# A hybrid block of linear attention, experts and sparse attention: swapped halves by transfer, GpSimd's order, straight code

## The chip, the cores and the metric

One core of one Trainium2 chip. The time is the device time of one execution in microseconds (us); lower is better. Engines: TensorE (PE; its weight load is shown as PEld), VectorE (DVE), ScalarE (ACT), GpSimd (POOL), SyncE (SP), which here only issues transfers.

## The reference, cut to what matters

Sixteen images of 256 tokens, width 128, float32. Four blocks with a residual each: linear attention, top-1 of 8 experts, sparse attention, the same experts. The change is in the sparse attention, of which this matters:

```python
Q, K, V = jnp.split(x @ w_qkv.T + b_qkv, 3, axis=-1)
Q, K = (_rope(Q), _rope(K))   # [x1*cos - x2*sin, x1*sin + x2*cos], x1 and x2 the halves
iq, ik, iw = ...              # index queries (4 heads), index keys, head weights
head_scores = relu(einsum('bqhd,bkd->bhqk', iq, ik))
index_scores = einsum('bhqk,bqh->bqk', head_scores, iw)
_, top_idx = jax.lax.top_k(index_scores, 32)
logits = einsum('bqd,bkd->bqk', Q, K) * scale + attn_bias   # -inf off top_idx
attn_out = softmax(logits) @ V
```

## The kernel before, in words

Each engine has its own program; semaphores order them. Stage one is the linear attention. Then the tokens are sorted by expert: the routing tables are worked out, 32 gathers on GpSimd's queue (L425) bring the rows in order, and 39 incidences (tile, expert) pass through the experts (`experts_tensor`, `experts_scalar`, `experts_vector`). Then comes the sparse attention, then routing and experts a second time.

The sparse attention is a pipeline over the 16 images, one step per image, its order written out by hand on each engine. In step s:

- TensorE: transposes of the normalised image s (L689), eight projections in four pairs (`project`, L658 and L661): two of index queries, index keys, q, q with its halves swapped, k, k swapped, and V times the output weights. Between them the transposed probabilities of image s-2 (L668). Then the product of probabilities and V of image s-2 (L722), index scores of image s (L677), logits of image s-1 (L732).
- ScalarE: evicts the projections (`projected`, L886; `vb`, L889), exponentials of image s-2 (L899), `prT` (L908), the head weights `iw` (L913), the next image's normalisation `xb` (L862), relu of the index scores (`rel`, L925), the first two heads times their weights (`part`, L932), the penalty `pen` of image s-1 from what the top-k left (L942).
- GpSimd: rotation of q and k of image s, as products with cosine (L479) and sine (L481) of 128x512 each and their sum `qr` (L486); `add_heads` for each of the two chunks (`head_sum`, L464); `inverse_std(s)`, which adds eps and takes the power (L456, L458) and gives `rs`; the output bias onto `X` (L491); `gather_x(s+3)`, two indirect transfers (L445).
- VectorE: for image s-1 the third and fourth head's share of the index scores (L1272, L1278) for chunks 0 and 1, with the masked logits of image s-2 (L1286) between; then four rounds of max (L1327) and match_replace (L1330), and beside them the output normalisation `xf` (L1260), `nb` (L1235), the division `attended` (L1248), statistics (L1208, L1215), and behind the last round the aggregates (L1227), which give `mv`.
- SyncE: two stores of 128 KB for an image as soon as `xf` and `x` are there (`store_rows`).

The names of the counters: `mv` is counted up once in VectorE's step s (after two steps ahead of image 0), and `inverse_std(u)` waits for `mv >= u + 3`, that is for the aggregates of step u. `hs` counts head sums, and L1272 waits for `hs >= C*b + c + 1` with b = s-1. `pje` counts evicted projections, `rp` the rotation's products, `qr` the rotated pairs, `S` the logits.

In this stage, in ScalarE's and VectorE's expert stages, and in SyncE's programs the middle steps are hardware loops (`steps` and `incidences` with `Fori`), whose counts are worked out in registers. TensorE's expert stage and GpSimd's attention stage are written out. `alone` is a wait followed by an increment of a counter nobody waits for.

## Time and profile before

| | us |
|---|---|
| median of three runs (lowest, highest) | 610.64 (608.79, 612.69) |
| the profiled execution: own time, span | 614.45, 612.6 |
| busy in the span: PE, DVE, ACT, POOL | 456.6, 381.5, 338.0, 285.5 |
| windows: linear attention and first routing | 0 to 106 |
| first expert stage, with its gathers | 106 to 238 |
| sparse attention | about 250 to 455 |
| in 340 to 350: PE, DVE, ACT, POOL busy, PE's granted clock | 9.64, 9.40, 8.67, 7.67 of 10.00, 1.00 |
| in 440 to 450: the same | 5.16, 8.17, 3.06, 0.93 of 10.00, 0.67 |
| second routing and expert stage | 455 to 612 |

The times of the timeline count from the start of the span. The profiled execution is one run; its own time stands beside its span since a little lies around the span. A granted clock of 1.00 is TensorE's full 2.4 GHz, 0.50 is 1.2 GHz, and values between are mixtures over the window.

### The profile page before, as it was taken

To read this page: it belongs to the slowest core of one execution; us is meant where nothing else is said; L and a number is where in the kernel's file an instruction comes from. 1 tells how busy PE (TensorE), PEld (TensorE's weight loads), DVE (VectorE), ACT (ScalarE), POOL (GpSimd) and SP (SyncE) were. 2 spreads that over 40 slices of the span, in tenths; PEclk is the share of its full clock that TensorE was granted. 3 is DMA by queue.
4 is the path that set the end of the run, shared out by engine and by line. 5 is a ranking of instruction groups with operands and counts; after the bars stand their busy time and mean duration, and the time that the engine had idled before them with its cause. 6 is when DMAs were issued, how large, how long until landed. Compare 5 with 4: busy or idle time off the path is not lost. (4 is left out here: it accounts for less than half of the span.)

```text
span 612.6 us, 12728 instructions
## 1 busy us (share of the span) xinstructions
PE 456.6 (75%) x3048; PEld 395.4 (65%) x3048; DVE 381.5 (62%) x1502; ACT 338.0 (55%) x935; POOL 285.5 (47%) x329
## 2 busy tenths in 40 slices
PE   1889958611989886899899899989648402999882
PEld 1688848511889886666667667667438402889881
DVE  6789967001565662189899999999957001555561
ACT  1668821201566651688988998998520201566660
POOL 5654421774000003587778778785410773044442
PEclk9989977855999998799999999999757955898996
DMA  8912221332011111001101001100110332001010
GB/s 249 312 54 71 77 79 3 103 103 69 5 32 33 31 31 32 9 15 30 28 27 53 26 26 41 37 27 18 36 35 2 104 107 65 2 32 32 31 32 17
DMA packets 45061, 32.32 MB, mean 53 GB/s; under 512 B 13524, under 2 KB 39508, under 8 KB 45012
## 3 DMA queue, kind: packets, MB, share of 16 engines
q1 hardware_dynamic: 39892, 19.11, 11.1%
q0 software_dynamic: 5120, 12.62, 7.5%
q8 instruction: 23, 0.38, 0.3%
q14 instruction: 26, 0.21, 0.1%
HBM read 19.10 MB, written 12.62 MB: 52 GB/s over the span
## 5 line engine op out<-in xcount | busy, mean ns | idle before, releaser
L637 PE MATMUL bank<-WE,hT 128*128 x624 | 90.9, 292 | 45.9 <-issue 27.8
L637 PEld LDWEIGHTS bank<-WE,hT 128*128 128x128 f32 x624 | 82.5, 206 | 48.8 <-issue 48.8
L627 PE MATMUL bank<-X,w 128*128 x624 | 89.0, 288 | 30.1 <-issue 29.3
L627 PEld LDWEIGHTS bank<-X,w 128*128 128x128 f32 x624 | 80.6, 202 | 33.5 <-issue 33.2
L1177 DVE TENSOR_SCALAR hT<-bank,w 128x128 f32<-128x128 f32 x156 | 47.6, 347 | 69.5 <-issue 35.6
L832 ACT ACTIVATE X<-bank 128x128 f32 (+1 forms) x64 | 17.8, 278 | 117.8 <-PE bank L618 66.0
L425 POOL DMA_INDIRECT big<-rows,gidx x64 | 61.0, 953 | 46.5 <-DVE gidx L1145 27.6
L445 POOL DMA_INDIRECT X<-x,pidx x32 | 31.6, 989 | 98.2 <-DMA x<-big 90.6
L658 PE MATMUL bank<-xbT,WB 128*128 128x256 f32 x224 | 63.0, 416 | 12.7 <-ACT xbT L870 8.8
L845 ACT ACTIVATE hT<-bank,w 128x128 f32<-128x128 f32 x156 | 48.6, 365 | 30.4 <-issue 17.2
L837 ACT ACTIVATE w<-WE 128x644 f32 x78 | 57.4, 736 | 4.3 <-DVE big L1189 3.7
L431 POOL DMA_INDIRECT out<-big,gidx x32 | 31.1, 972 | 59.9 <-DVE big L1189 59.4
L658 PEld LDWEIGHTS bank<-xbT,WB 128*128 128x128 f32 x224 | 41.9, 203 | 25.5 <-ACT iq L886 9.5
L1330 DVE MATCH_REPLACE8 wk<-m,wk 128x256 f32<-128x256 f32 x128 | 51.4, 410 | 0.0
L1183 DVE TENSOR_TENSOR yb<-bank,w 128x128 f32<-128x128 f32 x78 | 22.6, 289 | 44.7 <-remote 26.9
L1327 DVE MAX8 m<-wk 128x8 f32<-128x256 f32 x128 | 47.6, 413 | 0.0
L677 PE MATMUL bank<-ik,iq 64*128 64x256 f32 x256 | 38.0, 402 | 0.7 <-ACT big L925 0.7
L464 POOL TENSOR_TENSOR head_sum<-big 128x256 f32<-128x256 f32 x32 | 23.8, 743 | 29.7 <-ACT big L932 29.6
L1189 DVE SCALAR_TENSOR_TENSOR big<-yb,gm,big 128x128 f32 x78 | 27.5, 353 | 16.1 <-DVE yb L1183 11.4
L925 ACT ACTIVATE big<-bank 128x512 f32<-128x512 f32 x64 | 34.6, 591 | 1.1 <-PE bank L677 1.0
L512 PE MATMUL bank<-cst 128*128 128x128 f32 x188 | 28.1, 323 | 2.5 <-DVE big L1189 2.5
L886 ACT ACTIVATE big<-bank,COL 128x256 f32<-128x256 f32 x64 | 29.3, 492 | 1.1 <-PE bank L658 0.7
(163 smaller groups left out, 1032.1 us busy)
## 6 DMA issues: line engine op xcount, KB each, us to landing
WE<-w_experts SPq DMA_DIRECT2D x2, 2048.0 KB, 11.3
rows<-xf SPq DMA_DIRECT2D x32, 128.0 KB, 2.2
rows<-X SPq DMA_DIRECT2D x32, 128.0 KB, 2.5
X<-x SPq DMA_DIRECT2D x4, 512.0 KB, 6.5
x<-big SPq DMA_DIRECT2D x32, 64.0 KB, 1.5
big<-rows,gidx POOLq DMA_INDIRECT x64
WB<-w_idx SPq DMA_DIRECT2D x1, 640.0 KB, 5.2
WE<-b SPq DMA_DIRECT2D x1, 512.0 KB, 12.6
```

Source lines behind the costliest of these rows:

```text
L425: pool.indirect_dma_start(xg[:, j, :], None, rows_dram[n], bass.IndirectOffsetOnAxis(ap=gidx[:, j:j + 1], axis=0)).then_inc(f["g"][j % G_R ...
L445: pool.indirect_dma_start(X[:, t, :], None, x2_dram, bass.IndirectOffsetOnAxis(ap=pidx[:, t:t + 1], axis=0)).then_inc(b_["x"][r], 16)
L627: mm = pe.matmul(bank[r + 2 * (k // 2)][:, k % 2 * P:(k % 2 + 1) * P], w1[st.slot(1, 4)][:, k * P:(k + 1) * P], moving, start=True, stop=True)
L637: mm = pe.matmul(bank[4 + r][:, 0:D], hT[r][:, k, :], WE[:, bass.ds(expert[(s - 2) % TURN], 1), W2_AT + k * D:W2_AT + (k + 1) * D].rearran ...
L658: mm = pe.matmul(to, WB[:, i * D:(i + 1) * D], xbT[r][:, :], start=True, stop=True)
L677: mm = pe.matmul(bank[h % 2][:, h // 2 * S:(h // 2 + 1) * S], iq[r][lo:lo + IDX_DIM, h // 2, c * P:(c + 1) * P], ik[r][lo:lo + IDX_DIM, :] ...
L837: act.activation(w1[st.slot(0, 4)][:, :], WE[:, bass.ds(expert[st.base], 1), 0:W1_LEN].rearrange("p a w -> p (a w)"), ACT.Copy).then_inc(f ...
L845: act.activation(hT[r][:, k, :], bank[r][:, k * P:(k + 1) * P], ACT.Relu, bias=w1[st.slot(1, 4)][:, B1_AT + k:B1_AT + k + 1]).then_inc(f[" ...
L925: act.activation(rel[r][:, c, i::2, :], bank[i][:, :].rearrange("p (h k) -> p h k", h=2), ACT.Relu).then_inc(b_["rel"], 1)
L1177: dve.tensor_scalar(hT[r][:, k, :], bank[2 + r][:, k % 2 * P:(k % 2 + 1) * P], w1[st.slot(1, 4)][:, B1_AT + k:B1_AT + k + 1], 0.0, ALU.add ...
L1327: dve.max(m8[:, c, :], wk[r][:, c, :]).then_inc(b_["v"], 1)
L1330: dve.match_replace(wk[r][:, c, :], m8[:, c, :], wk[r][:, c, :], NEG).then_inc(b_["v"], 1)
```

## The change

Four things. The projections with swapped halves go: TensorE makes six instead of eight per image (index queries, index keys and q, k and V), in three pairs that alternate between two banks, and ScalarE evicts two fewer. SyncE copies the halves instead: after k is evicted, two transfers within SBUF write `qk[:, 0:2]` with upper and lower 64 partitions exchanged into `qk[:, 2:4]`. GpSimd's step has a new order: cosine product (into `qr`), `inverse_std(s)`, bias, gathers, head sum 0, wait for the transfers, sine product, sum, head sum 1. All loops named above but those of the linear attention and SyncE's first two are written out as straight code, and `alone` with a constant is only a wait. The weight table and the bias columns lose the swapped copies.

```diff
 def alone(eng, sem, count, passed):
-    if not isinstance(count, int) or count > 0:
+    if isinstance(count, int):
+        after(eng, sem, count)
+    else:
         eng.wait_ge(sem, count)
         eng.sem_inc(passed, 1)
...
         def incidences(eng, lag):
-            yield from (Step(s) for s in range(HEAD))
-            with eng.Fori(0, (T - HEAD) // TURN) as turn:
-                for k in range(TURN):
-                    yield Step(HEAD + k, TURN, turn)
-            yield from (Step(s) for s in range(T, NT + lag))
+            yield from (Step(s) for s in range(NT + lag))
...
-            for st in steps(sp, B, 0, 4, 2):
-                store_rows(1, st, 0, lambda b, r: X[:, tiles(b), :])
+            def turn_halves(b, r):
+                sp.wait_ge(b_["pje"], 6 * b + 5)
+                after(sp, b_["qr"], b - 1)
+                for lo in (0, P // 2):
+                    hi = P // 2 - lo
+                    sp.dma_start(qk[r][lo:lo + P // 2, 2:4, :], qk[r][hi:hi + P // 2, 0:2, :]).then_inc(b_["turn"][r], 16)
+            for st in (Step(s) for s in range(B + 4)):
+                if st.on(0, B):
+                    turn_halves(st.item(0), st.slot(0, 2))
+                if st.on(4, B):
+                    store_rows(1, st, 4, lambda b, r: X[:, tiles(b), :])
...
             for s in range(B + 2):
                 b, r = s, s % 2
                 if b < B:
-                    pool.wait_ge(b_["pje"], 8 * b + 7)
-                    pool.tensor_tensor(qk[r][:, 0:2, :], qk[r][:, 0:2, :], const("cos").unsqueeze(1).to_broadcast([P, 2, S]),
+                    pool.wait_ge(b_["pje"], 6 * b + 5)
+                    after(pool, b_["S"], C * (b - 1))
+                    pool.tensor_tensor(qr[r][:, :, :], qk[r][:, 0:2, :], const("cos").unsqueeze(1).to_broadcast([P, 2, S]),
                                        ALU.mult).then_inc(b_["rp"], 1)
-                    pool.tensor_tensor(qk[r][:, 2:4, :], qk[r][:, 2:4, :], const("sin").unsqueeze(1).to_broadcast([P, 2, S]),
-                                       ALU.mult).then_inc(b_["rp"], 1)
-                    add_heads(b, r, 0)
-                    pool.wait_ge(b_["rp"], 2 * (b + 1))
-                    after(pool, b_["S"], C * (b - 1))
-                    pool.tensor_tensor(qr[r][:, :, :], qk[r][:, 0:2, :], qk[r][:, 2:4, :], ALU.add).then_inc(b_["qr"], 1)
-                    add_heads(b, r, 1)
                 inverse_std(s)
...
                 if b + 3 < B:
                     gather_x(b + 3)
+                if b < B:
+                    add_heads(b, r, 0)
+                    pool.wait_ge(b_["turn"][r], 32 * (b // 2 + 1))
+                    pool.tensor_tensor(qk[r][:, 2:4, :], qk[r][:, 2:4, :], const("sin").unsqueeze(1).to_broadcast([P, 2, S]),
+                                       ALU.mult).then_inc(b_["rp"], 1)
+                    pool.wait_ge(b_["rp"], 2 * (b + 1))
+                    pool.tensor_tensor(qr[r][:, :, :], qr[r][:, :, :], qk[r][:, 2:4, :], ALU.add).then_inc(b_["qr"], 1)
+                    add_heads(b, r, 1)
```

On TensorE (the loops of ScalarE and VectorE are written out likewise):

```diff
-            for st in steps(pe, B, 4, 6, 2, ahead=1):
+            for st in (Step(s) for s in range(B + 4)):
...
-                    after(pe, b_["pje"], 8 * b + 2 * (pair - 1))
+                    after(pe, b_["pje"], 6 * b + 2 * (pair - 1))
...
-                        to = bank[2 + pair % 2][:, i % 2 * S:(i % 2 + 1) * S]
+                        to = bank[2 + (3 * st.slot(0, 2) + pair) % 2][:, i % 2 * S:(i % 2 + 1) * S]
...
                     project(1)
-                    project(2)
                 if st.on(2, B):
...
                     turn_probabilities(b, r, 0)
                 if st.on(0, B):
-                    project(3)
+                    project(2)
```

On ScalarE:

```diff
                 if st.on(0, B):
-                    projected(2)
+                    projected(2, (0,))
...
                 if st.on(0, B):
-                    projected(3)
-                    act.wait_ge(b_["pj"], 5 * (b + 1))
+                    projected(2, (1,))
+                    act.wait_ge(b_["pj"], 4 * (b + 1))
```

## Rows read from the trace of the kernel before

**Rows 1.** Timeline, ScalarE: start us, length us, line, tile, count, idle before.

```profile
345.13 0.60 ACT L908 ACTIVATE prT<-bank 128x512 f32<-128x512 f32 x1 [0.42 <-issue]
...
345.63 0.47 ACT L886 ACTIVATE big<-bank,COL 128x256 f32<-128x256 f32 x1
...
346.98 0.39 ACT L889 ACTIVATE vb<-bank 128x256 f32<-128x256 f32 x1 [0.88 <-PE bank L722]
...
358.75 0.39 ACT L889 ACTIVATE vb<-bank 128x256 f32<-128x256 f32 x1 [0.89 <-PE bank L722]
```

**Rows 2.** Timeline, TensorE, the same step.

```profile
344.63 0.38 PE L668 MATMUL bank<-cst,lg 128*128 128x128 f32 x2
...
345.79 1.16 PE L722 MATMUL bank<-vb,prT 128*128 128x128 f32 x8
```

**Rows 3.** Timeline, VectorE, one step.

```profile
330.06 0.48 DVE L1272 SCALAR_TENSOR_TENSOR wk<-big,iw,head_sum 128x256 f32<-128x256 f32 x1
330.45 0.48 DVE L1278 SCALAR_TENSOR_TENSOR wk<-big,iw,wk 128x256 f32<-128x256 f32 x1
...
331.19 0.80 DVE L1278 SCALAR_TENSOR_TENSOR wk<-big,iw,wk 128x256 f32<-128x256 f32 x1
331.91 0.74 DVE L1327 MAX8 m<-wk 128x8 f32<-128x256 f32 x2
...
340.16 0.38 DVE L1227 BATCH_NORM_AGGREGATE mv<-stat 128x2 f32<-128x6 f32 x4
340.86 0.91 DVE L1272 SCALAR_TENSOR_TENSOR wk<-big,iw,head_sum 128x256 f32<-128x256 f32 x1 [0.32 <-issue]
```

**Rows 4.** Timeline, GpSimd, one step.

```profile
338.40 0.72 POOL L464 TENSOR_TENSOR head_sum<-big 128x256 f32<-128x256 f32 x1 [1.57 <-ACT big L932]
339.08 1.27 POOL L486 TENSOR_TENSOR qr<-big 128x512 f32<-128x512 f32 x1
...
341.44 0.39 POOL L456 TENSOR_TENSOR vpe<-mv,eps 128x4 f32<-128x4 f32 x1
341.91 1.05 POOL L458 TENSOR_TENSOR rs<-vpe,mhalf 128x4 f32<-128x4 f32 x1
342.94 0.72 POOL L491 TENSOR_TENSOR X<-X,bo_bc 128x256 f32<-128x256 f32 x1
343.83 1.04 POOL L445 DMA_INDIRECT X<-x,pidx  x1 [0.17 <-issue]
345.17 0.95 POOL L445 DMA_INDIRECT X<-x,pidx  x1 [0.30 <-issue]
```

**Rows 5.** Page, DMA issues: count, KB each, us to landing.

```profile
rows<-xf SPq DMA_DIRECT2D x32, 128.0 KB, 2.2
```

**Rows 6.** Timeline, VectorE and GpSimd, start of the attention stage.

```profile
242.99 0.25 DVE L1227 BATCH_NORM_AGGREGATE mv<-stat 128x2 f32<-128x6 f32 x2
...
243.32 0.20 POOL L456 TENSOR_TENSOR vpe<-mv,eps 128x2 f32<-128x2 f32 x1 [1.93 <-DVE mv L1227]
243.59 0.73 POOL L458 TENSOR_TENSOR rs<-vpe,mhalf 128x2 f32<-128x2 f32 x1
```

**Rows 7.** Timeline, ScalarE, GpSimd and VectorE, first image.

```profile
252.01 1.35 ACT L886 ACTIVATE big<-bank,COL 128x256 f32<-128x256 f32 x3 [0.71 <-PE bank L658]
...
259.00 0.78 POOL L464 TENSOR_TENSOR head_sum<-big 128x256 f32<-128x256 f32 x1
...
259.82 0.48 DVE L1272 SCALAR_TENSOR_TENSOR wk<-big,iw,head_sum 128x256 f32<-128x256 f32 x1 [0.62 <-POOL head_sum L464]
```

**Rows 8.** Timeline, VectorE and TensorE, last image and tail.

```profile
436.25 0.48 DVE L1272 SCALAR_TENSOR_TENSOR wk<-big,iw,head_sum 128x256 f32<-128x256 f32 x1
...
449.88 2.07 PE L722 MATMUL bank<-vb,prT 128*128 128x128 f32 x8 [0.69 <-ACT prT L908]
```

**Rows 9.** Page, DMA queues; and timeline, VectorE, second expert stage.

```profile
q8 instruction: 23, 0.38, 0.3%
...
504.42 0.29 DVE L1183 TENSOR_TENSOR yb<-bank,w 128x128 f32<-128x128 f32 x1 [16.19 <-remote]
```

More of the change, by code:

```diff
@@ L282, in build @@
                "idx", "rel", "prt", "hs", "s1", "wk", "v", "pen", "S", "ttr", "exp", "PT", "prT", "PV",
-               "pinv", "xo")} | {"x": sems("b_x", 2)}
+               "pinv", "xo")} | {"x": sems("b_x", 2), "turn": sems("b_turn", 2)}
         def xrows(dram, b, lo, hi):
@@ L589, in route_tensor @@
                     pe.wait_ge(b_["row"], 1)
[L590 to L591 removed]
+                    pe.matmul(bank[3][:, 0:D], bv_rep[:, :], WB[:, 5 * D:6 * D], start=True, stop=True)
+                    pe.matmul(bank[4][:, 0:D], WB[:, 6 * D:7 * D], WB[:, 5 * D:6 * D], start=True, stop=True).then_inc(b_["wvo"], 1)
                 keep_clock(KEEP_ROUTE, bank[2][:, 0:P])
@@ L712, in _ @@
                         mm = pe.matmul(bank[5][:, S + c * IDX_HEADS:S + (c + 1) * IDX_HEADS], xbT[r][:, c * P:(c + 1) * P],
-                                       WB[:, 9 * D:9 * D + IDX_HEADS], start=False, stop=(c == C - 1))
+                                       WB[:, 7 * D:7 * D + IDX_HEADS], start=False, stop=(c == C - 1))
                     mm.then_inc(b_["pj"], 1)
@@ L800, in _ @@
                     xf_out(0, st.item(5), st.slot(5, 2), bank[6][:, 0:S])
-            act.activation(bv_rep[:, :], ones, ACT.Copy, scale=COL[:, 9:10]).then_inc(b_["row"], 1)
+            act.activation(bv_rep[:, :], ones, ACT.Copy, scale=COL[:, 7:8]).then_inc(b_["row"], 1)
             def route_exp(n, k):
@@ L873, in _, with projected @@
             turned(0, 0)
-            for st in steps(act, B, 4, 6, 2, ahead=1):
+            for st in (Step(s) for s in range(B + 4)):
                 b, r = st.item(0), st.slot(0, 2)
-                def projected(pair):
-                    act.wait_ge(b_["pj"], 5 * b + pair + 1)
-                    for i in (2 * pair, 2 * pair + 1):
-                        src = bank[2 + pair % 2][:, i % 2 * S:(i % 2 + 1) * S]
+                def projected(pair, which=(0, 1)):
+                    act.wait_ge(b_["pj"], 4 * b + pair + 1)
+                    for i in (2 * pair + w for w in which):
+                        src = bank[2 + (3 * r + pair) % 2][:, i % 2 * S:(i % 2 + 1) * S]
                         if i == 3:
-                            after(act, b_["qr"], b - 1)
-                        if i < 7:
-                            dst = iq[r][:, i, :] if i < 2 else ik[r][:, :] if i == 2 else qk[r][:, (0, 2, 1, 3)[i - 3], :]
+                            after(act, b_["rp"], 2 * (b - 1))
+                        if i < 5:
+                            dst = iq[r][:, i, :] if i < 2 else ik[r][:, :] if i == 2 else qk[r][:, i - 3, :]
                             act.activation(dst, src, ACT.Identity, bias=COL[:, 2 + i:3 + i]).then_inc(b_["pje"], 1)
@@ L1267, in _ @@
             shifts(Step(0), 0)
-            for st in steps(dve, B, 3, 6, 2, ahead=2):
+            for st in (Step(s) for s in range(B + 3)):
                 def add_third(c):
@@ L1352 @@
     wt = a["L0_attn_b_w_qkv"].T
-    other = np.r_[D // 2:D, 0:D // 2]
     wiq, wik = a["L0_attn_b_w_iq"].T, a["L0_attn_b_w_ik"].T
@@ L1356 @@
     wiw[:, :IDX_HEADS] = a["L0_attn_b_w_iw"].T
-    w_idx = np.concatenate([wiq, wik, wik, wt[:, :D], wt[:, :D][:, other], wt[:, D:2 * D], wt[:, D:2 * D][:, other],
-                            a["L0_attn_b_w_o"].T, a["L0_attn_b_w_qkv"][2 * D:], wiw], axis=1)
+    w_idx = np.concatenate([wiq, wik, wik, wt[:, :D], wt[:, D:2 * D], a["L0_attn_b_w_o"].T, a["L0_attn_b_w_qkv"][2 * D:], wiw], axis=1)
     bq, bk, bv = np.split(a["L0_attn_b_b_qkv"], 3)
@@ L1361 @@
     cols = np.stack([a["L0_attn_a_gamma"].reshape(D), a["L0_attn_a_beta"].reshape(D), biq[:D], biq[D:],
-                     np.concatenate([bik, bik]), bq, bq[other], bk, bk[other], bv], axis=1)
+                     np.concatenate([bik, bik]), bq, bk, bv], axis=1)
     w1 = a["L0_ffn_W1"].transpose(1, 0, 2)
```

9 lines of the change are left out of this document (4 added, 5 removed).

## The prediction

> **What bounds the kernel now.** The view by windows puts the sparse-attention stage at about 250 to 455 us, with TensorE at full clock in most of it (the small table above). Its 16 images run as a pipeline, one step per image, so I read one step engine by engine in the timeline, looking for what each engine waits for. ScalarE evicts `vb` at 346.98 and again at 358.75: a step is 11.8 us. In it ScalarE stands still twice, for the turned probabilities (start 345.13) and for 0.88 us before `vb`, which waits for TensorE's product of probabilities [rows 1]. TensorE in turn reaches that product at 345.79 only after the transpose at 344.63, and ScalarE must evict that first [rows 2]. So the loop is ScalarE's queue with this piece of TensorE's in it, 11.8 us long. VectorE is the near rival: from its third product for chunk 1 (330.06) to the end of the statistics (340.16 + 0.38 = 340.54) it is hardly ever idle [rows 3]. GpSimd has slack, but its place in the order matters below: it makes both head sums of image s (the first at 338.40), and only then the inverse deviations (341.44, 341.91), the bias sum (342.94) and the two gathers (343.83, 345.17) [rows 4]. The inverse deviations wait for `mv`, which VectorE gives at the very end of its step s, behind all four rounds of max and match.
>
> **Part by part.**
>
> *Two projections fewer.* Each image loses two 128x256 products on TensorE and two evictions on ScalarE; one of these is the 0.47 us at 345.63 [rows 1]. Both evictions lie in the gaps where ScalarE waits for TensorE anyhow. The eviction of k now waits for the V product, so `prT` could come about 0.1 us later. On the old loop this is worth -0 to +0.1 us a step, and that loop is no longer the bound (below). I take 0.
>
> *The transfers.* SyncE issues two of 128 KB (64 partitions of 2 KB each) for each image once k is evicted. The nearest row is the store of one image, 128 KB, 2.2 us from issue to landing [rows 5]. The sine product comes some 13 us after k's eviction in the new order (below), so they are hidden; they would show only above 13 us. On SyncE's queue the store of image s-4 now stands behind k of image s. Its data are ready before that and its buffer is wanted again only in the next step: nothing. At the tail the stores go without any transfer ahead of them.
>
> *GpSimd's order.* Now: cosine product, inverse deviations(s), bias sum, gathers, head sum 0, sine product, sum, head sum 1. The head sums of image s, which VectorE needs for the first operations of its step s+1, thus stand behind a wait for `mv` from the end of VectorE's step s. Before, they stood ahead of that wait. This closes a ring: VectorE's whole step, then GpSimd's whole chain, then VectorE's next step. Nothing overlaps any more except the cosine product. What queues behind the wait on GpSimd is everything listed; who waits for it is VectorE (third product), and through it ScalarE and TensorE.
>
> The ring, from rows. VectorE: third product of chunk 1 at 330.06 to the end of the aggregates at 340.54, 10.48 us. The fourth product of chunk 1 took 0.80 us there, with GpSimd running, and its sister 0.48; the max followed 0.72 us after its start, where 0.40 is the pitch of the uncontended ones. GpSimd will be idle at that point, so minus 0.32: **10.16 us** [rows 3]. From `mv` to GpSimd's start: 242.99 + 0.25 = 243.24 to 243.32, 0.08 us [rows 6]. GpSimd: from 341.44 to the end of the second gather 345.17 + 0.95 + about 0.05, 4.73 us; head sum 0.68 (the pitch 338.40 to 339.08); sine product 1.27 (as the sum of the same shape at 339.08) plus 0.07 for a wait on its own result (243.32 + 0.20 to 243.59 [rows 6]); sum 1.27 less 0.03 of overlap; head sum 0.72: **8.71 us** [rows 4]. Hand-over to VectorE, from 259.00 + 0.78 to 259.82: 0.04 us [rows 7]. Sum 10.16 + 0.08 + 8.71 + 0.04 = **19.0 us a step**, where it was 11.8.
>
> There are 15 such turns between the third product of chunk 1 of the first image and that of the last. Ten (s = 3 to 12) are full: 190.0. Three (13 to 15) have no gather, 2.34 less: 16.7; the last two of them also have two-column deviations (0.5 less) and less statistics (estimated at 0.5): 15.7 each. Turn 1 has no divide, no `xf`, half of the statistics (estimated at 2.1 from the lengths of the like) and narrow deviations: 16.4. Turn 2 lacks `xf`, 0.6: 18.4. Sum 190.0 + 16.7 + 2 x 15.7 + 16.4 + 18.4 = 272.9 us.
>
> Its start: k of image 0 is evicted at about 252.5 (the fifth product, the first of the three at 252.01 [rows 7], instead of the seventh), the cosine product ends at 253.8, then 4.3 us of the narrow chain, 0.7, 1.3, 1.2, 0.7: VectorE starts at 262.0, against 259.82 [rows 7]. So it reaches the last image's third product at 262.0 + 272.9 = 534.9, before at 436.25 [rows 8]: **+98.7 us**. Behind it the tail runs as before.
>
> *Is another ring longer?* With 19 us a step TensorE works less than half of the time, and in the tail of before it stood at half clock, the product of probabilities taking 2.07 instead of 1.16 us [rows 2, 8]. With these lengths I followed ScalarE and TensorE from VectorE's masked logits: that product ends 5 to 6 us behind, VectorE wants it at 6.8; both parts of the head sums are there by 14 us, GpSimd asks for them at 15 and 18.3. So a low clock costs 0 here; from a delay of 1 us more it would begin to show.
>
> *Straight code.* In the old loop VectorE lost 0.32 us at each return, seen at 340.86 [rows 3]. In the attention stage this now lies inside its wait: 0. In each of the two expert stages VectorE has three turns: at most 2 x 2 x 0.32 = -1.3 us, and about -0.6 if half is hidden behind TensorE. `alone` loses an increment; max follows max at the pitch of other instructions, so 0. Against this, more instructions must be brought in: the instruction queues moved 23 packets in one of them before, and during the gathers ahead of the experts VectorE stood for 16.19 us with nothing in the trace to show for it [rows 9]. If that is code coming in behind the gathers, more code could lengthen it; if not, nothing. Bounds -1.3 and +20; I take -1, since the work at that place was straight code already.
>
> *The skill, weighed.* [Rows 3] show a product with two inputs in SBUF at 0.48 us alone and 0.80 to 0.91 beside GpSimd. The Trainium skill, SBUF — State Buffer, "SBUF: two separate sides", says that VectorE and GpSimd share one port pair as an exclusive lock; the trace agrees, and by it the new order even saves VectorE that much, the 0.32 us taken off above. The Trainium skill, Runtime: NRT & Kernel Launch, "Instruction fetch mechanics", says that a branch taken out of the two pages at hand forces a fetch, and so speaks for straight code; the row shows 0.32 us at a return, so by the trace there is little to win.
>
> **Forecast.** The profiled execution took 614.45 us, 3.8 above the median of 610.64, which I start from: 610.6 + 98.7 - 1 = 708 us.
>
> **Rivals.**
> 1. *A second ring or slow code adds to it.* The low clock makes the products late by more than the 1 us of slack, or code arrives late on VectorE or behind the gathers. For: the stalls of [rows 9] and the half clock of [rows 8]. Price: 1 to 2 us in 15 turns, or 5 to 20 once: 720 to 745. Chance 0.17.
> 2. *The ring is shorter.* Operations on GpSimd or VectorE that were slowed by each other run faster now, or my estimate of the start is late: 0.5 to 1.5 us a turn, 685 to 698. For: only VectorE's two-input operations show contention in the rows; GpSimd's lengths are all alike. Chance 0.12.
> 3. *Not slower.* It decides at one point: whether `mv` of step s is there before GpSimd needs it. If GpSimd ran a whole step behind, its wait would be over when it comes to it, and ScalarE's ring would stay: 11.8 + 0.1 a step with the stage's two fewer products, 610 us, or 600 if ScalarE's gaps closed. Against it: VectorE cannot start step s+1 without head sums s, and these stand behind `mv` s, so nobody can be ahead. Chance 0.02, half of it faster.
> 4. *The transfer is the bound.* It would need more than 13 us against 2.2 [rows 5]; each us beyond adds 15: 725 for one. Chance 0.02.
>
> The forecast itself (699 to 718) has 0.67. Below 692 or above 730 I leave some 0.15, so the range is 692 to 730. The three runs of before spread by 0.6%, so about 1% is what a measurement can tell. Faster 0.01, same 0.01, slower 0.98.
>
> **What would show it.** VectorE's third product waits about 8 us for `head_sum` in each step, and GpSimd's deviations wait for `mv`, with GpSimd going from them through gathers and head sums without a gap; step length 19.0 us, 16.7 or less in the last three; the sine product waits for no transfer; ScalarE and TensorE idle for some 9 us a step, TensorE's granted clock falls. Wrong would be a step of 12 us, a wait of VectorE for ScalarE instead, or a sine product that waits for DMA. The expert stages should keep their length within 2 us each.

## The result and the profile after

The changed kernel takes **704.06 us** (median of 4 runs, 702.65 to 704.28), the kernel before 611.66 (4 runs beside them, 608.79 to 613.18): ratio 1.151, with an interval of 1.146 to 1.156. It is 15% slower. The profiled execution took 703.98 us with a span of 702.2; that of before took 614.45 with 612.6.

VectorE in one step of the attention stage, from the timeline of the changed kernel (start, length, line, tile, idle before). It answers to [rows 3].

```profile
379.45 0.38 DVE L1238 BATCH_NORM_AGGREGATE mv<-stat 128x2 f32<-128x6 f32 x4
385.27 1.40 DVE L1283 SCALAR_TENSOR_TENSOR wk<-big,iw,head_sum 128x256 f32<-128x256 f32 x1 [5.44 <-POOL head_sum L473]
...
388.51 0.48 DVE L1283 SCALAR_TENSOR_TENSOR wk<-big,iw,head_sum 128x256 f32<-128x256 f32 x1 [1.50 <-POOL head_sum L473]
...
391.49 1.00 DVE L1271 TENSOR_SCALAR xf<-X,mv,rs 128x128 f32<-128x128 f32 x2
...
398.51 0.38 DVE L1238 BATCH_NORM_AGGREGATE mv<-stat 128x2 f32<-128x6 f32 x4
```

Where [rows 3] ran on from the aggregates into the next step, VectorE now stands for 5.44 us, works for some 1.8, and stands for 1.50 more, both times for a head sum. The third product of chunk 1 starts at 388.51 and in the neighbouring steps at 369.45 and 407.57: **a step is 19.06 us**.

GpSimd in the same step, the answer to [rows 4]:

```profile
379.91 0.20 POOL L465 TENSOR_TENSOR vpe<-mv,eps 128x4 f32<-128x4 f32 x1 [6.81 <-DVE mv L1238]
380.19 1.05 POOL L467 TENSOR_TENSOR rs<-vpe,mhalf 128x4 f32<-128x4 f32 x1
381.23 0.71 POOL L494 TENSOR_TENSOR X<-X,bo_bc 128x256 f32<-128x256 f32 x1
382.11 1.04 POOL L454 DMA_INDIRECT X<-x,pidx  x1 [0.17 <-issue]
383.45 0.95 POOL L454 DMA_INDIRECT X<-x,pidx  x1 [0.30 <-issue]
384.43 0.73 POOL L473 TENSOR_TENSOR head_sum<-big 128x256 f32<-128x256 f32 x1
385.11 1.27 POOL L501 TENSOR_TENSOR big<-big,cst 128x512 f32<-128x512 f32 x1
386.46 1.33 POOL L504 TENSOR_TENSOR qr<-qr,big 128x512 f32<-128x512 f32 x1
387.75 0.72 POOL L473 TENSOR_TENSOR head_sum<-big 128x256 f32<-128x256 f32 x1
390.88 1.27 POOL L489 TENSOR_TENSOR qr<-big,cst 128x512 f32<-128x512 f32 x1 [2.41 <-ACT big L897]
```

It begins 0.08 us behind the aggregates (379.83) and runs from `vpe` to the second head sum with no idle time but the gathers' own; 0.04 us behind that head sum (388.47) VectorE starts. Each engine waits while the other works. The sine product (385.11) waits for no transfer.

The view that adds up the waits, from 240 to 540 us: who waited for whom, us in total, times, the longest.

```profile
DVE wk L1283 <- POOL head_sum L473: 106.9, 32, 9.7
POOL vpe L465 <- DVE mv L1238: 101.9, 15, 7.5
...
ACT lg L910 <- DVE lmin L1297: 69.3, 29, 5.2
POOL qr L489 <- ACT big L897: 38.5, 15, 4.9
```

The first two are the ring, seen from its two ends: 106.9 us of VectorE's (9.7 and 1.8 of them before the first turn) and 101.9 of GpSimd's. ScalarE's and TensorE's waits are the ring's echo. On the page, the granted clock and the transfers:

```profile
PEclk9999869559999996688777797776795595589997
...
big<-big SPq DMA_DIRECT2D x32, 128.0 KB, 2.4
```

The transfers land in 2.4 us, near the 2.2 of the stores in [rows 5]. In the attention stage the clock is below 0.8 of full speed in most slices, and in most steps TensorE's product of probabilities shows the length that it has at the half clock, as in [rows 8], where [rows 2] have 1.16:

```profile
392.44 2.06 PE L732 MATMUL bank<-vb,prT 128*128 128x128 f32 x8
```

It cost nothing: VectorE never waited for it, and the step in which this product took 1.14 us (410.96) is 19.05 us long all the same.

**Where the 89.6 us of span come from.** Cut both timelines at two points, the aggregates of the first image and the last third product of chunk 1.

| | before | after | difference |
|---|---|---|---|
| start to the first image's `mv` | 249.20 | 244.15 | -5.05 |
| from there to the last third product | 187.05 | 287.67 | +100.6 |
| from there to the end | 176.35 | 170.38 | -6.0 |

So the ring cost 100.6 us and everything outside it gave back 11.0. These are two single executions; the other pair of traces, b0 and a0 below, gives +102.0 and -5.4. From the first third product of chunk 1 (257.46) to the last (531.82) are 274.4 us in 15 turns; the last three turns, which have no gather, took 16.5, 15.6 and 15.5.

### The profile page after: what moved, and what is told of

Read it like the earlier page. It is cut to its first block and busy times, and to the rows that moved or that the text cites. A ratio compares the mean times of both kernels' runs of the same rounds, so it can differ in the third digit from the quotient of the medians.

```text
span 702.2 us, 11429 instructions
## 1 busy us (share of the span) xinstructions
PE 481.4 (69%) x2984; PEld 410.7 (58%) x2984; DVE 391.7 (56%) x1501; ACT 330.5 (47%) x902; POOL 284.9 (41%) x329
## 5 line engine op out<-in xcount | busy, mean ns | idle before, releaser
L648 PE MATMUL bank<-WE,hT 128*128 x624 | 87.9, 286 | 47.4 <-issue 35.0
L1283 DVE SCALAR_TENSOR_TENSOR wk<-big,iw,head_sum 128x256 f32<-128x256 f32 x32 | 31.3, 978 | 106.9 <-POOL head_sum L473 106.9
L679 PE MATMUL bank<-cst,lg 128*128 128x128 f32 x64 | 20.0, 415 | 76.8 <-ACT lg L910 76.8
L843 ACT ACTIVATE X<-bank 128x128 f32<-128x128 f32 x64 | 17.8, 279 | 115.2 <-PE bank L629 87.7
L856 ACT ACTIVATE hT<-bank,w 128x128 f32<-128x128 f32 x156 | 48.6, 366 | 27.3 <-issue 17.5
L679 PEld LDWEIGHTS bank<-cst,lg 128*128 128x128 f32 x64 | 8.6, 189 | 87.0 <-issue 69.3
L669 PE MATMUL bank<-xbT,WB 128*128 128x256 f32 x160 | 49.6, 448 | 9.9 <-ACT xbT L881 9.8
L465 POOL TENSOR_TENSOR vpe<-mv,eps 128x4 f32<-128x4 f32 (+1 forms) x20 | 4.1, 206 | 118.0 <-DVE mv L1238 118.0
L688 PE MATMUL bank<-ik,iq 64*128 64x256 f32 x256 | 48.2, 497 | 4.5 <-ACT big L936 4.5
L910 ACT ACTIVATE lg<-lg,lmin 128x256 f32<-128x256 f32 x32 | 16.3, 511 | 70.9 <-DVE lmin L1297 70.9
L669 PEld LDWEIGHTS bank<-xbT,WB 128*128 128x128 f32 x160 | 32.6, 222 | 15.9 <-ACT xbT L881 12.0
## 6 DMA issues: line engine op xcount, KB each, us to landing
WE<-w_experts SPq DMA_DIRECT2D x2, 2048.0 KB, 11.7
```

The costliest lines, as they stand in the source:

```text
L648: mm = pe.matmul(bank[4 + r][:, 0:D], hT[r][:, k, :], WE[:, bass.ds(expert[(s - 2) % TURN], 1), W2_AT + k * D:W2_AT + (k + 1) * D].rearran ...
L669: mm = pe.matmul(to, WB[:, i * D:(i + 1) * D], xbT[r][:, :], start=True, stop=True)
L688: mm = pe.matmul(bank[h % 2][:, h // 2 * S:(h // 2 + 1) * S], iq[r][lo:lo + IDX_DIM, h // 2, c * P:(c + 1) * P], ik[r][lo:lo + IDX_DIM, :] ...
L856: act.activation(hT[r][:, k, :], bank[r][:, k * P:(k + 1) * P], ACT.Relu, bias=w1[st.slot(1, 4)][:, B1_AT + k:B1_AT + k + 1]).then_inc(f[" ...
L1283: dve.scalar_tensor_tensor(wk[r][:, c, :], rel[r][:, c, 2, :], iw[r][:, c, 2:3], head_sum[r][:, c, :], ALU.mult, ALU.add).then_inc(b_["s1" ...
```

## The experiments

**Three things could explain the 100 us**: the order on GpSimd that makes head sums wait for `mv` (my theory), the transfers (a rival), or a second ring through ScalarE and TensorE (a rival). And the 11 us given back called for tests of their own. Kernels of one group ran on one chip beside runs of the kernel before. The chips are not alike: on two of them (groups 1 and 2) the kernel before takes 537 us, on the others 611. Only ratios, and differences within a group, are compared below; the absolute times in the expectations of e1, e2, e3 and e5 were meant for the slower chips. All the kernels compute the whole reference. In the diffs a minus is the changed kernel and a plus the experiment, unless it is said otherwise.

**Group 1** (before: 537.19, 23 runs): e1, e2, e4, e7. **Group 2** (before: 537.51, 17 runs): e3, e5, e6.

### e1: the old order of head sums, all else changed

GpSimd's whole second half goes back behind the second head sum; transfers, six projections and straight code stay.

```diff
-                inverse_std(s)
-                ... bias sum ...
-                    gather_x(b + 3)
                 if b < B:
                     add_heads(b, r, 0)
                     ... sine product, sum ...
                     add_heads(b, r, 1)
+                inverse_std(s)
+                ... bias sum ...
+                    gather_x(b + 3)
```

> The changed kernel with GpSimd's old order: cosine product, head sum 0, wait for the transfers, sine product, sum, head sum 1, and only then the inverse deviations, the bias and the gathers. Transfers, six projections and straight code stay. Theory of the ring (VectorE's step and GpSimd's chain in series, because the head sums stand behind the wait for mv): the step falls from 19.06 to 11.8 to 12.0 us and the time to 603 to 610 us. Rival, that the transfers or the waits for them cost the time: it stays above 690 us. A smaller form of it: the transfer now has no work in front of it but one head sum, and each us of waiting that shows on VectorE adds 16 us.

**536.10 us, ratio 0.997** (0.994 to 1.000). The whole loss is gone with the transfers still there. Most steps are 11.96 us long, some 12.2 to 14.1 (from one eviction of `vb` to the next, as in e6 and e8 to e10). Two losses that the kernel before did not show in this form, from VectorE's timeline:

```profile
304.03 2.20 DVE L1271 TENSOR_SCALAR xf<-X,mv,rs 128x128 f32<-128x128 f32 x2
...
359.36 0.49 DVE L1219 BATCH_NORM_STATS2 stat<-X 128x6 f32<-128x128 f32 x2 [1.52 <-DMA X<-x,pidx]
```

GpSimd in those two steps, and then SyncE in the second:

```profile
303.89 0.95 POOL L454 DMA_INDIRECT X<-x,pidx  x1 [0.30 <-issue]
304.87 1.27 POOL L489 TENSOR_TENSOR qr<-big,cst 128x512 f32<-128x512 f32 x1
...
352.97 1.04 POOL L454 DMA_INDIRECT X<-x,pidx  x1 [0.17 <-issue]
354.31 0.95 POOL L454 DMA_INDIRECT X<-x,pidx  x1 [0.30 <-issue]
```

```profile
353.39 1.15 SPq L367 DMA_DIRECT2D big<-big  x2
354.58 0.59 SPq L340 DMA_DIRECT2D rows<-xf  x1
```

`xf`, 0.59 us long in the kernel before, where only a gather runs beside it (345.31 beside 345.17 of [rows 4]), started 0.14 us into a gather and ended 0.09 us behind the cosine product that followed. And the rows of a gather issued at 354.31 were waited for until 359.36, with the transfers' packets and the store's issued around them. e9 and e10 take these two apart.

### e2: one line moved back

Of the new order, only the inverse deviations return to the end.

```diff
-                inverse_std(s)
                 if b < B:
                     pool.wait_ge(b_["xb"], b + 1)
                     ... bias sum, gathers, head sums, sine product, sum ...
+                inverse_std(s)
```

> The changed kernel with one call moved: the inverse deviations go behind head sum 1; bias and gathers stay in front of head sum 0 and the sine product. If the ring is closed by the wait for mv alone, this one line gives everything back: step 11.8 to 12.0 us, 603 to 610 us. If it is the quantity of work in front of the sine product (bias and two gathers, 3.2 us) that costs, the time stays some 45 us above the kernel before, 650 us or more.

**538.42 us, ratio 1.001** (0.999 to 1.004). Bias sum and gathers still stand ahead of the head sums, and the loss is gone all the same. So the ring is closed by **one wait**, that of the deviations for `mv`. GpSimd's timeline, where `vpe` no longer waits at all:

```profile
340.79 0.72 POOL L473 TENSOR_TENSOR head_sum<-big 128x256 f32<-128x256 f32 x1
341.47 0.39 POOL L465 TENSOR_TENSOR vpe<-mv,eps 128x4 f32<-128x4 f32 x1
...
344.80 1.27 POOL L489 TENSOR_TENSOR qr<-big,cst 128x512 f32<-128x512 f32 x1 [1.81 <-ACT big L897]
```

A step is 12.27 us, 0.45 over the old one; two are longer, 14.1 and 13.2 (more on them under e10). In most, `xf` takes 1.79 us (345.04 to 346.83) beside the cosine product and the bias sum, 1.2 more than alone.

### e3: the order alone, in the kernel before

Eight projections, both halves on TensorE, loops as before; only the order on GpSimd is the new one (a minus is the kernel before).

```diff
-                    ... sine product, head sum 0, sum, head sum 1 ...
                 inverse_std(s)
                 ... bias sum, gathers ...
+                if b < B:
+                    add_heads(b, r, 0)
+                    ... sine product, sum ...
+                    add_heads(b, r, 1)
```

> The kernel before with GpSimd's new order alone: cosine product, inverse deviations, bias, gathers, head sum 0, sine product, sum, head sum 1; eight projections, no transfers, loops as before. Theory of the ring: step 19 to 19.2 us and 700 to 712 us, since nothing else of the change is on that ring. Rival, that the slowdown needs the transfers or the straight code: 612 to 620 us.

**635.32 us, ratio 1.181** (1.176 to 1.187): +98 us from the order alone, with no transfer in the kernel. A step is 18.8 us. The two ends of the ring, on GpSimd:

```profile
384.66 0.20 POOL L456 TENSOR_TENSOR vpe<-mv,eps 128x4 f32<-128x4 f32 x1 [5.22 <-DVE mv L1228]
...
392.49 0.72 POOL L464 TENSOR_TENSOR head_sum<-big 128x256 f32<-128x256 f32 x1
...
397.01 1.27 POOL L479 TENSOR_TENSOR big<-big,cst 128x512 f32<-128x512 f32 x1 [3.79 <-ACT big L887]
```

The chain is 8.55 us (384.66 to 393.21), as in the changed kernel. The cosine product comes later here, behind eight projections, and so does not meet `xf`, which takes 0.59 us (at 396.23), 0.41 less than in the changed kernel: enough for the difference between 18.8 and 19.06.

### e5: a smaller dose

The deviations stay ahead of the head sums, bias sum and gathers go behind them.

```diff
                 inverse_std(s)
-                ... bias sum, gathers ...
                 if b < B:
                     add_heads(b, r, 0)
                     ... sine product, sum ...
                     add_heads(b, r, 1)
+                ... bias sum, gathers ...
```

> The dose: the changed kernel with the inverse deviations alone in front of head sum 0; bias and gathers go behind head sum 1. The ring stays closed but is shorter by bias and gathers: 10.38 us of VectorE, 0.08, then 0.28 + 1.04 + 0.68 + 1.35 + 1.29 + 0.72 = 5.36 us of GpSimd, 0.04: 15.9 us a step where it is 19.06, and 704 - 13 x 3.2 - 3 x 0.7 = 660 us. If the order mattered otherwise than by such a sum, the step would be 12 or 19 us.

**598.71 us, ratio 1.114** (1.109 to 1.119). The ring is there with a shorter chain on GpSimd:

```profile
393.69 0.20 POOL L465 TENSOR_TENSOR vpe<-mv,eps 128x4 f32<-128x4 f32 x1 [6.83 <-DVE mv L1238]
...
398.33 0.72 POOL L473 TENSOR_TENSOR head_sum<-big 128x256 f32<-128x256 f32 x1
...
402.20 1.29 POOL L489 TENSOR_TENSOR qr<-big,cst 128x512 f32<-128x512 f32 x1
```

From 393.69 to 399.05 are 5.36 us, 3.2 less than in the changed kernel, as the sum of the moved rows had it. The step averages some 16.6 us where I had expected 15.9 (in time, 61 us lost where my 660 us stood for 48): the chain is right, and VectorE's part is 0.76 too long. Of that, 0.32 is `xf` at 1.32 us instead of 1.00, beside the cosine product (402.20), and 0.45 the third product at 399.08, which took 0.93 beside the bias sum where [rows 3] have 0.48.

### e4: the straight code alone

The kernel before with the loops written out and with `alone` as a plain wait for a constant count, and nothing else (a minus is the kernel before; `alone` and the like lines of TensorE, ScalarE and SyncE are not shown).

```diff
-            yield from (Step(s) for s in range(HEAD))
-            with eng.Fori(0, (T - HEAD) // TURN) as turn:
-                for k in range(TURN):
-                    yield Step(HEAD + k, TURN, turn)
-            yield from (Step(s) for s in range(T, NT + lag))
+            yield from (Step(s) for s in range(NT + lag))
...
-            for st in steps(dve, B, 3, 6, 2, ahead=2):
+            for st in (Step(s) for s in range(B + 3)):
```

> The kernel before with straight code alone, projections and order as they were. By my prediction the loops cost 0.32 us at a return of VectorE, most of it hidden: 0 to -2 us. What the changed kernel's trace suggests: it ran 2.3 us less up to the attention stage and 5.5 us less behind it, and if straight code is the cause this kernel is 6 to 9 us faster than before, with the attention step unchanged at 11.8 us. If those 8 us came by chance from run to run, or from something else in the change, it stays within 2 us of before.

**528.11 us, ratio 0.983** (0.979 to 0.986): 9.1 us gained, where my sum had 1. It is the fastest of all versions. Its attention steps are 11.82 us long, as before.

### e7: e2 with the experts in loops again

The first hunk of e4's diff, the other way round, applied to e2. So e2 against e7 is the experts' straight code alone.

> As the kernel with the deviations last, but ScalarE's and VectorE's expert stages are hardware loops again. If straight code in the expert stages is what saves the 8 us outside the attention stage, this one is 5 to 9 us slower than the kernel with the deviations last; if not, they are within 2 us of each other.

**544.26 us, ratio 1.014** (1.009 to 1.018), 5.8 us over e2. From the first to the last weight row of the experts the two stages take 79.6 and 78.1 us with loops, 76.4 and 76.0 without: 5.3 of the 5.8. VectorE at such a turn, first in e2, then in e7:

```profile
143.36 0.16 DVE L1180 TENSOR_TENSOR gm<-big,mine 128x1 f32<-128x1 f32 x1 [2.16 <-PE bank L638]
143.50 0.61 DVE L1188 TENSOR_SCALAR hT<-bank,w 128x128 f32<-128x128 f32 x2
```

```profile
144.18 0.16 DVE L1184 TENSOR_TENSOR gm<-big,mine 128x1 f32 x1 [2.49 <-PE bank L642]
144.46 0.61 DVE L1192 TENSOR_SCALAR hT<-bank,w 128x128 f32<-128x128 f32 x2
```

With the loop VectorE starts its first operation 0.33 us later, and then 0.14 more pass before its second. The view puts the wait down to TensorE, but in e7 TensorE had long been done with this product:

```profile
142.65 1.06 PE L642 MATMUL bank<-X,w 128*128 x8
```

It ends at 143.71, 0.47 us before VectorE starts; in e2 the two are 0.14 us apart. So the delay is **VectorE's own**, 0.47 us to its second operation where [rows 3] show 0.32. With three turns in each stage the 5.3 us are 0.9 a turn on average, but they are not alike. Against the same weight rows of e2, ScalarE falls behind by 0.4, 0.5 and 2.2 us at the three turns of the first stage and by 0.5, 0.8 and 0.5 at those of the second. At the one of 2.2 us TensorE's clock fell as well, to 0.62 from 164 to 166 us; the product that takes 1.15 us at the same place in e2 took 1.83:

```profile
164.17 1.83 PE L642 MATMUL bank<-X,w 128*128 x8
```

In e3, which has the same loops, the clock stays full there, and this third turn costs 0.7 us. So a turn costs 0.4 to 0.8 us, and the rest of e7's loss, some 1.5 us, is this fall of the clock.

### e6: the third pair of projections ahead of the transposes

e2, with `project(2)` back at its old place on TensorE (a minus is e2).

```diff
                     project(0)
                     project(1)
+                    project(2)
                 ... turn_probabilities(b, r, 0) ...
-                if st.on(0, B):
-                    project(2)
```

> The kernel with the deviations last, and on TensorE the third pair of projections (k and V) in front of the first transposes of the probabilities instead of behind them. It tests what bounds the step when the ring is open: by my reading ScalarE waits for the transposes and then for the product of probabilities, and TensorE stands idle before them. If so, prT comes up to 0.8 us earlier, the step falls from 11.9 to 11.0 to 11.3 us, and the time by 8 to 13 us against the kernel with the deviations last. If VectorE is already the bound, it stays within 3 us of it.

**534.91 us, ratio 0.994** (0.991 to 0.998), some 4 us better than e2 by the two ratios to the kernel before; I had expected 8 to 13. Steps are 11.8 us with two at 12.5 to 12.65, and `xf` is still long (1.43). The step fell by 0.47 us against e2, and 0.36 of that is `xf`, at 1.43 instead of 1.79, since the cosine product now starts earlier. The eviction of k that came late was a part of what kept e2 back, and less than half of what I had counted on.

**Group 3** (before: 611.52, 23 runs): a0, b0, e8, e9; and **e10** on one more chip (before: 611.14, 17 runs). It asks two things: whether the results hold where the kernel before takes 611, and why no version with six projections gets past 0.994.

### a0 and b0: the changed kernel and the kernel before, again

> The changed kernel itself, on the chip of the experiments, where the kernel before takes 537 us and not 611. The ring has no part in what differs between the chips: steps of 19.06 us again, so 537 + 98.7 less 5.8 to 9 for straight code = 627 to 632 us. If the slowdown were a factor of the whole (1.151), it would be 618 us, and the steps shorter.

**706.1 us, ratio 1.150** (1.144 to 1.157). The absolute number that I had expected was that of the faster chips; it ran on one of the others. The ratio is that of the result, and steps are 19.06 us again:

```profile
387.36 1.40 DVE L1283 SCALAR_TENSOR_TENSOR wk<-big,iw,head_sum 128x256 f32<-128x256 f32 x1 [5.43 <-POOL head_sum L473]
...
390.60 0.48 DVE L1283 SCALAR_TENSOR_TENSOR wk<-big,iw,head_sum 128x256 f32<-128x256 f32 x1 [1.50 <-POOL head_sum L473]
```

> The kernel before itself, for its trace on this chip. Two accounts of the 74 us by which it is faster here: if TensorE's clock or all engines are faster, the attention step is shorter than 11.8 us; if it is the standing still of all engines behind the 32 gathers at the start of each expert stage, the step is 11.8 us as before, each expert stage is 35 to 38 us shorter, and no wait of 10 us without a cause stands in it.

**612.31 us** (one run). Its attention steps are 11.8 us, as on the faster chips; the difference is in the expert stages, 115.2 and 118.5 us long here, 78.3 and 79.8 in e3, which has the same loops and ran on a faster chip. VectorE behind the first stage's gathers:

```profile
134.42 0.29 DVE L1183 TENSOR_TENSOR yb<-bank,w 128x128 f32<-128x128 f32 x1 [14.23 <-remote]
...
152.68 0.61 DVE L1177 TENSOR_SCALAR hT<-bank,w 128x128 f32<-128x128 f32 x2 [17.32 <-issue]
```

These stand beside the 16.19 us of [rows 9]. In e3 and e4, on the faster chips, no such wait is found. The 37 and 39 us in the two stages account for all of the 74 us between the chips. So my question whether more code would lengthen those waits has an answer: not by anything seen. The same VectorE waits are 9.21 and 20.80 us in the trace of before and 8.51 and 21.17 in that of after, and the stages are shorter after (113.4 and 113.0) than before (115.9 and 118.2).

### e8: `xf` on ScalarE

e6, with the normalised output computed by ScalarE from a bias that VectorE prepares; it relieves VectorE's queue (a minus is e6).

```diff
-                for c in range(C):
-                    ins = dve.tensor_scalar(xf[r][:, c, :], one_tile(b, c), mv2[u][:, C + c, 0:1],
-                                            rs2[u][:, C + c:C + c + 1], ALU.subtract, ALU.mult)
+                dve.scalar_tensor_tensor(nbx[r][:, :], mv2[u][:, C:2 * C, 0], -1.0, rs2[u][:, C:2 * C],
+                                         ALU.mult, ALU.mult).then_inc(b_["nbx"], 1)
...
+                        ins = act.activation(xf[e][:, c, :], X[:, d * C + c, :], ACT.Identity,
+                                             scale=rs2[u][:, C + c:C + c + 1], bias=nbx[e][:, c:c + 1])
```

> The kernel with the third pair of projections first, and xf of the output side made by ScalarE behind prT, with a 0.15 us product on VectorE for its bias. There xf took VectorE 1.43 us a step beside GpSimd's cosine product. If VectorE's queue, with this wait for the shared port in it, bounds the step of 11.8 us, the step falls to 11.0 to 11.4 us and the time by 5 to 12 us, to 523 to 530 us. If ScalarE's ring bounds it, the 0.8 us added there fill its wait of 1.31 us before vb and the step stays at 11.8 us or grows by up to 0.3.

**609.92 us, ratio 0.996** (0.993 to 1.000), no better than e6. ScalarE's timeline:

```profile
340.31 0.60 ACT L919 ACTIVATE prT<-bank 128x512 f32<-128x512 f32 x1
341.62 0.88 ACT L928 ACTIVATE xf<-X,nbx,rs 128x128 f32<-128x128 f32 x2 [0.71 <-DVE nbx L1280]
342.40 0.36 ACT L900 ACTIVATE vb<-bank 128x256 f32<-128x256 f32 x1
```

ScalarE now does the 0.88 us of work and waits 0.71 for the bias, which VectorE makes no sooner: its tiny operation takes 0.60 to 0.79 us beside the cosine product, where the like one behind it (`nb`, 341.51) takes 0.15. Steps are 11.8 to 12.7, but for one of 13.5. That VectorE's queue as such bounds these versions is not borne out: relieving it moved the wait.

### e9: the cosine product later

e1, with the cosine product waiting for V's eviction too, so that it starts behind `xf`.

```diff
-                    pool.wait_ge(b_["pje"], 6 * b + 5)
+                    pool.wait_ge(b_["pje"], 6 * b + 6)
```

> The kernel with the old order of GpSimd, transfers and six projections (536.1 us), with one number changed: the cosine product waits for the eviction of V's product too and so starts behind VectorE's xf. If the collision of these two costs the 8 us by which that kernel is behind the one with straight code alone (528.1 us), xf takes 0.59 us in every step, the steps are 11.8 us throughout and the time is 528 to 532 us. If the transfers cost them by making the gathers land late, the waits of VectorE for gathered rows stay and so do 534 to 538 us.

**609.17 us, ratio 0.994** (0.991 to 0.998). `xf` is 0.59 us in every step, with a gather still beside it (353.62), so its 2.2 us in e1 did come from the cosine product. Yet steps are 11.7 to 12.5: seven of them wait for gathered rows, as here.

```profile
353.75 0.59 DVE L1271 TENSOR_SCALAR xf<-X,mv,rs 128x128 f32<-128x128 f32 x2
...
371.05 0.49 DVE L1219 BATCH_NORM_STATS2 stat<-X 128x6 f32<-128x128 f32 x2 [1.25 <-DMA X<-x,pidx]
```

The traces say more on this wait. In e4, with the same place of the gathers in GpSimd's order and no transfers, VectorE reads the rows 3.45 to 3.81 us behind the issue of the last gather and waits for them for 0.26 us at most. The twelve waits of e1 and e9 are up to 1.66 us, and but for one they end 3.8 to 5.2 us behind it; in ten of them the trace shows the transfers issued 0.8 to 1.0 us ahead of that gather. So the rows come late where transfers and gathers meet, which is argued from these rows and not from a run of its own.

### e10: the gathers first of all

TensorE as in e6; GpSimd: bias sum, gathers, cosine product (behind V's eviction), head sum 0, sine product, sum, head sum 1, deviations.

```diff
-                ... cosine product (for pje >= 6 * b + 5) ...
-                inverse_std(s)
                 if b < B:
                     ... bias sum ...
                 if b + 3 < B:
                     gather_x(b + 3)
                 if b < B:
+                    pool.wait_ge(b_["pje"], 6 * b + 6)
+                    ... cosine product ...
                     add_heads(b, r, 0)
                     ... sine product, sum, head sum 1 ...
+                inverse_std(s)
```

> Drawn from the others: the third pair of projections first on TensorE, and GpSimd in the order bias, gathers, cosine product (behind the eviction of V's product and so behind xf), head sum 0, sine product, sum, head sum 1, deviations last. No ring through mv, the gathers early enough, xf at 0.59 us. If the wait for the shared port was what held the step at 11.8 us, it falls to 11.3 to 11.6 us and the ratio to the kernel before to 0.97 to 0.98, as good as straight code alone (0.983) or better. If the chain of head sums, masked logits and exponentials bounds it, or TensorE's clock falls for want of work, the step is 11.8 to 12.1 us and the ratio 0.985 to 0.995.

**606.47 us, ratio 0.993** (0.991 to 0.996). No gather is late, since each is issued a whole step ahead of where e9 has it, and `xf` is 0.59 us; steps are 11.8 in part and 12.0 to 12.66 in the rest. What is left is seen in the view by windows (us; busy time of each engine; granted clock, DMA share, GB/s), here e10:

```profile
300.00:320.00 20.00, 17.58 (x100) 13.06 (x100) 19.34 (x80) 15.04 (x43) 14.88 (x16) 0.91 0.25 67
320.00:340.00 20.00, 17.12 (x103) 12.97 (x104) 18.01 (x75) 16.95 (x47) 16.71 (x18) 1.00 0.14 35
```

and the same stretches of e4, with eight projections:

```profile
300.00:320.00 20.00, 18.51 (x115) 14.15 (x115) 19.30 (x82) 17.37 (x50) 15.54 (x17) 1.00 0.17 41
320.00:340.00 20.00, 17.93 (x108) 13.99 (x110) 18.70 (x77) 17.39 (x50) 16.53 (x19) 1.00 0.15 37
```

Over 280 to 380 us TensorE is busy for 17.5 of 20 us in e10 and 18.1 in e4; the granted clock is full in all five windows of e4, and in e10 it is 0.91 in two and 0.96 in one. Step by step the falls of the clock can be priced. In three steps of e10 the product of probabilities takes 2.06, 1.39 and 1.80 us where it takes 1.14 in the others, here the last of them:

```profile
363.07 1.80 PE L730 MATMUL bank<-vb,prT 128*128 128x128 f32 x8
```

From third product to third product these three steps last 13.17, 12.76 and 13.18 us, 3.7 us over 11.8 each; all 15 steps take 178.45 us in e10 and 174.59 in e4. In size, the falls of the clock account for nearly all by which e10 is behind e4 in this stage. The long steps of e2 (product 2.05 us) and e6 (1.76) are of the same kind. No such step stands in e4 or in the kernel before (its last images left out), and none in e9, which has six projections too: there the clock is full in all five windows with TensorE busy for 16.2 of 20 us. So less work on TensorE does not by itself bring the fall; what does is open. What bounds the open ring at 11.8 us in e4 as in the kernel before was not changed by any of these edits, and is not settled.

## Why the prediction was right, and where its sizes were off

Predicted 708 us (692 to 730), measured 704.06. By its own steps:

**The order closes a ring: right, and shown.** e3 has the order alone and loses 98 us; e2 takes one wait out of the ring and is level with the kernel before; e5 shortens GpSimd's chain by 3.2 us and the step by some 2.5. The point on which the third rival hung, that nobody can be a step ahead, holds: `vpe` waits for `mv` in each full step, 6.81 us in the one shown. The wait of VectorE that I had put at about 8 us is 6.9, in two parts.

**The step, 19.0 us: 19.06.** Its terms were off in both directions. VectorE: 10.16 predicted, 10.38 measured (388.51 to 398.89); `xf` at 1.00 us instead of 0.59, since in the new order it runs beside the cosine product. I had followed the two engines' overlap for the products of [rows 3], and not for the one operation that would newly overlap. Hand-over: 0.08 both. GpSimd: 8.71 predicted, 8.56 measured (379.91 to 388.47); `vpe` took 0.20 us, as in [rows 6], where I had taken the 0.39 of [rows 4]. It was long there because VectorE ran beside it, and in the ring VectorE stands still; rival 2 had called GpSimd's lengths all alike. Second hand-over: 0.04 both. That the sum is right to 0.06 us is partly luck: +0.22 on one engine and -0.15 on the other.

**Fifteen turns, 272.9 us: 274.4.** The short turns at the end (16.7, 15.7, 15.7) came out at 16.5, 15.6, 15.5; the first, with its estimated parts (16.4), at 17.0.

**Its start, 262.0: 257.46.** The whole stage began 5.05 us earlier, and the way from the first `mv` to this product was 0.5 longer than I had it. Counted from the first `mv`, the ring cost +100.6 where I had +98.7.

**Transfers hidden: right for this kernel.** 2.4 us, and no wait of the sine product. It is less plain where the ring is open: there the late gathers of e1 and e9 stand beside the transfers (353.39 between two gathers at 352.97 and 354.31). In e10, where the transfers are issued beside the gathers too but the gathers come earlier in GpSimd's order, there are none. By e4, which has none of these waits above 0.26 us, the transfers delay the rows; no run has moved the transfers alone.

**Two projections fewer are worth nothing: right.** No version with six of them is better than 0.993, and e4 with eight has 0.983. What they cost back is in sight: `xf` beside the cosine product (0.36 us a step between e2 and e6), late rows, and steps in which the clock falls (3.7 us in e10).

**A low clock costs 0: right.** 2.06 us for the product of probabilities, and every wait in the ring ends with VectorE or GpSimd. The product ends at 394.50, and VectorE asks for it at 395.55, so the slack of about 1 us that I had is there too. One premise was wrong: TensorE is not busy for less than half of the time but for 14.01, 13.66 and 11.18 of 19.06 us in the three steps from 369.45 on, with the clock at 0.68, 0.77 and 0.86, since its work takes longer at the lower clock.

**Straight code, -1: the wrong size.** The step that failed: "In each of the two expert stages VectorE has three turns: at most 2 x 2 x 0.32 = -1.3 us". The gain is 9.1 us by e4 and 11.0 and 5.4 by the two pairs of traces outside the ring, against bounds of -1.3 and +20. 5.8 of it is in the experts by e7. I had counted two returns a stage at 0.32 us; the runs show three places a stage at 0.4 to 0.8 us each, VectorE's own delay being 0.47, and one fall of the clock on top. My sign that the expert stages keep their length within 2 us failed with it: they are 2.5 and 5.2 us shorter. Of the other 3.3 us of e4, 0.6 to 0.7 lie between the first statistics of the attention stage and the `mv` of the first image (7.1 us in before, b0 and e3, 6.4 in e4); the rest was not traced. The Trainium skill, Runtime: NRT & Kernel Launch, "Instruction fetch mechanics", speaks for straight code since taken branches force fetches; I had weighed it down by the one row, and the runs agree with its direction. The error is 8 to 10 us, under 1.5% of the time, and was partly cancelled by the ring's +1.9: that the total came within 4 us is partly luck too.

**The stall as a price of more code: not seen.** The waits of [rows 9] are nearly as long after as before, and are absent from e3 and e4 on the faster chips.

## What to carry to other kernels

Before moving an instruction ahead on an in-order engine, list what its wait then stands in front of, and ask whether the engine that ends the wait needs any of it first: if so, the two work in turn, and the step is the sum of both chains (11.8 us became 19.06 with hardly any work added). Such a ring can be summed from the old trace to 1%, if each operation's length is taken from a row where the same neighbour runs beside it, or none does. Price a loop at every turn, its last included, and measure the delay from the end of the work that was waited for: the releaser that a view names may have been done for some time (0.47 us in e7).

## What the runs showed of the hardware

**Small VectorE operations beside GpSimd's.** `xf` (two 128x128 in fp32) takes 0.59 us alone or beside a gather (e3, e9). Beside GpSimd's product it takes 1.00 (the changed kernel) and 1.32 (e5), beside product and sum 1.79 (e2), and 2.20 where it began beside a gather with the product right behind (e1). A 128x2 operation goes from 0.15 to between 0.60 and 0.79 (e8). In the other direction `vpe` falls from 0.39 to 0.20 us when VectorE stands still. The Trainium skill, SBUF — State Buffer, "SBUF: two separate sides", tells of a port pair that the two engines share by an exclusive lock; these rows agree with it in kind, on operations that I had not counted. In e1 one of the two operations of `xf` alone took 1.95 us, longer than any one operation of GpSimd beside it (1.27).

**Chips differ by 74 us in this kernel.** They differ behind the bursts of 32 gathers ahead of the experts, where on some chips VectorE stands for up to 21 us and ScalarE for up to 24 us at a time, 37 to 39 us a stage in all, and on two chips not at all; steps of the attention stage are equal on both. The cause is open: the trace names nothing that ends these waits.

**A short fall of the granted clock costs about 1 us of a step.** In e10 three steps with the product of probabilities at 2.06, 1.39 and 1.80 us instead of 1.14 are 13.17, 12.76 and 13.18 us long instead of 11.8. Without the ring, and ahead of the last images, they were seen in this stage only in versions with six projections (e2, e6, e7, e8, e10), but not in all of these (e9); that the missing work brings them is not shown.
